# Two-layer conditioned sequence kernel: the second half of the next batch's query and key projection moved into a batch's last two half-steps

## The chip, the cores and the metric

The kernel runs on one core of a Trainium2 chip. The metric is the device time of one execution in microseconds (us); less is better. The engines are TensorE (PE, weight loads PEld), VectorE (DVE), ScalarE (ACT), GpSimd (POOL) and SyncE (SP, which here only issues DMAs). They run their own instruction streams and meet only at semaphores.

## The reference, cut to what matters

x is (8, 512, 256), the condition t is (8, 64). Two layers follow each other:

```python
# layer 0
scale = cond @ norm_w.T + 1.0
h = x * (scale * rsqrt(mean(x * x) + EPS))
val, gate = split(h @ up_w.T)
h = val * gelu(gate)
hq, wq = act_quant(h), weight_quant(down_w)
x = hq @ wq.T + x
# layer 1, attention: 16 heads of 16
n = gamma * rmsnorm(x) + beta
q, k, v = n @ W_q.T, n @ W_k.T, n @ W_v.T          # split into heads
x = x + a_alpha * (softmax(scale * q @ k.T) @ v) @ W_o.T
# layer 1, feed-forward
n = gamma * rmsnorm(x) + beta
x = x + f_alpha * (silu(n @ gate_w.T) * (n @ hidden_w.T) @ out_w.T + out_b)
```

## The kernel before

Every fp32 product outside layer 0's second one is made of three matmuls: each operand is split into a high part (rounded to fp32r) and a low part (the rest), and high x high, high x low and low x high are summed in PSUM (PARTS, L40). ScalarE writes the high parts, VectorE or GpSimd subtracts to get the low ones.

**Phase 1** (up to about 260 us) runs layer 0 over 32 tiles of 128 tokens, and leaves x and its normalised, transposed form (xa) in DRAM. It also makes the first half of batch 0's query and key stacks.

**Phase 2** is what the change touches. It goes over the 8 batches. The body of a batch is written once for each engine (`pe_batch`, `act_batch`, `dve_batch`, `pool_batch`, `sp_batch`); batch 0 is unrolled, batches 1 to 5 are a loop, 6 and 7 are unrolled. A batch has 32 half-steps (HALVES). In half-step h TensorE does (`excursion_pe`): two score matmuls of the batch (`score_pe`, L927) and, for maxima needed 11 half-steps later, one pair of raw score matmuls (`raw_pe`, L886), whose row maxima VectorE takes (`maximum_dve`, L894). The next raw pair waits until the last maximum is read. In even half-steps the four matmuls of values follow (`values_pe`, L946), which need ScalarE's exps (`exp_act`, L935) of the two half-steps before. A group of four heads takes 8 half-steps; its maxima go, negated, into rows of `q_stack` by 8 small DMAs (`shift_dve`, `shift_sp`).

Behind that a half-step does one or two entries of a table (`plan`, L1187): the attention of batch b is interleaved with the feed-forward of batch b - 1 and projections. Before the change the table of a looped batch is: half-step 0, query and key projection of the second half of this batch's heads (L812); 1 and 4, the two parts of v (L862); 2 and 3, the output product of batch b - 1's attention (`wo_pe`, L1007); 7, transposes of its normalised rows (`xf_pe`, L1075); 8 and 9, query and key projection of the first half for batch b + 1; 10 to 25, gate and hidden products alternating (L1113); 26 to 31, the output product (`out_pe`, L1157) in 8 half pieces of 12 matmuls. The last batch keeps the pieces of the last two of these half-steps for after its last values.

The table entries share two PSUM banks, `ab[0]` and `ab[1]`. Semaphores `pair_full` and `pair_free` count their uses; `uses` (L1207) works out which use each entry is, and every engine waits for that count.

A projection's result goes bank, ScalarE high part (`qk_act`, L819), VectorE low part (`qk_dve`, L826) into a staging buffer, and from there by 12 DMAs of 128 KB into `q_stack` and `k_stack`. The staging of the first half is in `split`, that of the second half in the last two slots of `hid`, which the feed-forward uses too (RESERVED, L794). SP issues 8 of the 12 DMAs, ScalarE's queue 4 (`stack_sp`, `stack_act`).

The chain between the output product and xf is: VectorE scales and adds the residual (L1017, L1027), ScalarE squares (L1034), VectorE the mean (L1041), GpSimd the power -1/2 (L1045), VectorE the four normalised rows (`normed_dve`, L1059), TensorE transposes, VectorE gamma and beta (L1085), ScalarE and GpSimd the parts (L1092, L1098). The next batch's input is split by ScalarE and GpSimd (L535, L549) at half-step 5. An engine does in half-step h the follow-up work of the table entries of h - 1. On VectorE the follow-ups that free a bank come ahead of the maximum, others behind it.

In batch 0 empty odd half-steps get three filler matmuls (`fill_pe`, L1227).

Of the kernel before, what the change touches and what calls it, by code (L numbers as in the profile page):

```python
# [5 lines left out]
def cond_seq_kernel(nc, x_tok, xT, condT, vec_wT, up_wT, down_wT, wqT, wkT, wvT, woT, gate_wT, hidden_wT,  # L6
# [40 lines left out]
    with ctx:  # L47
# [653 lines left out]
        def before_act(act, n):  # L701
# [9 lines left out]
            for w in range(2):  # L711
                if n == QK_AT[w] + 1:
                    act.wait_ge(alpha_stored, 16)
                    qk_act(act, 0, w, 0, psum[6 + w])
# [16 lines left out]
        def before_pe(pe, n):  # L731
# [4 lines left out]
            for w in range(2):  # L736
                if n == QK_AT[w]:
                    pe.wait_ge(par_ready, 2)
                    pe.wait_ge(alpha_done, 3)
                    qk_pe(pe, 0, 0, w, 0, psum[6 + w])  # L740
# [4 lines left out]
        def before_dve(dve, n):  # L745
# [8 lines left out]
            for w in range(2):  # L754
                if n == QK_AT[w] + 1:
                    qk_dve(dve, 0, w, 0, psum[6 + w])
# [37 lines left out]
        RESERVED = NH - 2  # L794
# [11 lines left out]
        def qk_pe(pe, c, m, w, use, bank=None):  # L806
            bank = ab[w] if bank is None else bank
            pe.wait_ge(q_in_low, credited(q_in_low, c + 1))
            pe.wait_ge(pair_free[w], credited(pair_free[w], use))
# [4 lines left out]
            last.then_inc(pair_full[w], 1)  # L814

        def qk_act(act, m, w, use, bank=None):
            bank = ab[w] if bank is None else bank
# [4 lines left out]
        def qk_dve(dve, m, w, n, bank=None):  # L822
            bank = ab[w] if bank is None else bank
            dve.wait_ge(qk_high, n + w + 1)
            high, low = staging(m, w)
            nc.vector.scalar_tensor_tensor(low, bank[:], SOFTMAX_SCALE if w == 0 else 1.0, high.bitcast(f32),  # L826
                                           ALU.mult, ALU.subtract).then_inc(pair_free[w], 1)


        def stack_dma(eng, m, w, half, r):  # L830
# [3 lines left out]
                          .bitcast(f32), staging(m, w)[part][64 * half:64 * half + 64, :].bitcast(f32)) \  # L834
                .then_inc(stacked[m], 16)

        def stack_sp(sp, m, uses, scores=None):

            for w, rows in ((0, range(ROWS // HD)), (1, range(ROWS // HD - 2))):
                sp.wait_ge(pair_free[w], credited(pair_free[w], uses[w] + 1))  # L840
                if scores is not None:
                    sp.wait_ge(score_full, scores)
                for r in rows:
# [3 lines left out]
        def stack_act(act, m, half, use, scores=None):  # L847

            act.wait_ge(pair_free[1], credited(pair_free[1], use + 1))
            if scores is not None:  # L850
                act.wait_ge(score_full, scores)
# [4 lines left out]
        def v_pe(pe, c, m, use):  # L856
            pe.wait_ge(q_in_low, credited(q_in_low, c + 1))
            pe.wait_ge(pair_free[m], credited(pair_free[m], use))
            for t in range(HALF):
                tok = (m * HALF + t) * P  # L860
                for i, (a, wp, k) in enumerate(PROJECTION):
                    last = nc.tensor.matmul(ab[m][:, t * D:(t + 1) * D], xa_part[a][:, k, tok:tok + P],  # L862
                                            wv[wp][:, k, :], start=(i == 0), stop=(i == 5))
            last.then_inc(pair_full[m], 1)
# [72 lines left out]
        def values_pe(pe, b, g, kt, v_use=None):  # L937

            if v_use is not None:
                m = kt // HALF  # L940
                pe.wait_ge(pair_free[m], credited(pair_free[m], v_use[m] + 1))
# [175 lines left out]
        def gate_act(act, c, f, use, spare=False):  # L1117
            act.wait_ge(pair_full[0], use + (f + 1))
            if f > 0:
                act.wait_ge(pair_free[1], credited(pair_free[1], use + f))  # L1120
# [7 lines left out]
        def product_dve(dve, c, f, use, spare=False):  # L1128
            dve.wait_ge(pair_free[0], credited(pair_free[0], use + (f + 1)))
            dve.wait_ge(prod_low, credited(prod_low, c * NH + f))  # L1130
            dve.wait_ge(pair_full[1], use + (f + 1))
# [3 lines left out]
        def product_act(act, c, f, use, staged):  # L1135
            if f == RESERVED:
                act.wait_ge(stacked[1], staged * STACK)
# [9 lines left out]
        def out_pe(pe, c, t, half, use):  # L1147
# [11 lines left out]
            if t % HALF == HALF - 1 and half == 1:  # L1159
                last.then_inc(pair_full[m], 1)  # L1160

        def out_dve(dve, c, m, use):
# [4 lines left out]
                                    fscale[:].unsqueeze(1).broadcast_to([P, HALF, D]), ALU.mult).then_inc(pair_free[m], 1)  # L1167
# [9 lines left out]
        V_AT, WO_AT, XF_AT, FFN_AT, OUT_AT = (1, 4), 2, 7, 10, 26  # L1177
        Q_AT, K_AT, TO_STACK = 8, 9, 16
# [438 lines left out]
```

## Time and profile before

| | |
|---|---|
| runs, median (lowest to highest) | 1056.83 us of 3 (1056.44 to 1062.42) |
| profiled execution, time | 1055.76 us |
| its span | 1054.0 us |
| TensorE busy | 996.8 us, 95% |
| VectorE busy | 761.7 us, 72% |
| ScalarE busy | 536.2 us, 51% |
| GpSimd busy | 269.4 us, 26% |
| share of TensorE's full clock granted, mean | 0.968 |

The busy times say how long an engine had an instruction in it; the matmuls are pipelined, so a busy TensorE may still be held up. The page's chain of waits, followed back from the end, lies on TensorE for 78% of the span and on VectorE for 12%. The median lies 1.07 us above the profiled execution's own time.

### The profile page before, as it was taken

Reading aid. Unit: us, or ns where it says so; the run is one execution under the profiler, and the core shown is the slowest. Engines: PE = TensorE matmul, PEld = TensorE weight load, DVE = VectorE, ACT = ScalarE, POOL = GpSimd, SP = SyncE. Lnnn points to the kernel's source line nnn. Section 1 sums busy time; section 2 is a strip of 40 time slices with the busy share of each in tenths; the row PEclk is TensorE's granted clock in tenths of the full one; section 3 lists DMA queues with packets and bytes.
Section 4 is the critical chain, followed back from the end, with each engine's and each line's share of the span. In section 5 each row is a group of like instructions: output and inputs, shape, how many; then the busy total and the mean of one; then the engine's idle time right before and its main releaser. Section 6 shows DMA issues by size and latency. Waiting matters only on the chain.

```text
span 1054.0 us, 17114 instructions
## 1 busy us (share of the span) xinstructions
PE 996.8 (95%) x5402; PEld 618.3 (59%) x5402; DVE 761.7 (72%) x1214; ACT 536.2 (51%) x1119; POOL 269.4 (26%) x258
## 2 busy tenths in 40 slices
PE   6999999996999899989989998999899899989988
PEld 4777777773534455645655564556456555645677
DVE  5888788996577777678677767776875877587233
ACT  5466455453555555456445545554564555356421
POOL 1365422221000312132122213221321232122142
PEclk9999999997999899989999998999899899999999
DMA  9544574432420240313022212403130222120000
GB/s 288 144 104 128 141 155 116 120 95 71 111 62 7 59 113 2 81 50 66 11 70 68 47 34 63 98 1 80 51 66 11 72 65 32 62 51 7 11 16 21
DMA packets 93718, 75.11 MB, mean 71 GB/s; under 512 B 44881, under 2 KB 79769, under 8 KB 93665
## 3 DMA queue, kind: packets, MB, share of 16 engines
q1 hardware_dynamic: 79072, 57.20, 20.9%
q10 hardware_dynamic: 14592, 17.25, 7.2%
q8 instruction: 27, 0.44, 0.2%
q14 instruction: 27, 0.21, 0.1%
HBM read 27.73 MB, written 12.61 MB: 38 GB/s over the span
## 4 chain that ended last, share of the span: by engine, by line
PE 78%; DVE 12%; issue 4%; DMA 2%; SPq 1%; ACT 1%; POOL 0%; DVEq 0%; ACTq 0%; POOLq 0%
PE bank L1113 19%; PE bank L362 12%; PE bank L927 10%; PE bank L946 10%; PE bank L1157 8%; PE raw_pair L886 6%; PE bank L812 4%; DVE rowmax L894 3%; PE bank L1007 2%; DVE amax L444 2%; PE bank L385 1%; PE bank L1075 1%; PE bank L862 1%; DVE h L414 1%; DVE x_in L1059 1%
## 5 line engine op out<-in xcount | busy, mean ns | idle before, releaser
L894 DVE TENSOR_REDUCE rowmax<-raw_pair 128x2 f32<-128x1024 f32 x256 | 312.9, 1222 | 127.7 <-PE raw_pair L886 127.7
L935 ACT ACTIVATE probs<-bank 128x512 f32<-128x512 f32 x512 | 281.8, 596 | 230.0 <-PE bank L927 227.7
L886 PE MATMUL raw_pair<-k_stack,q_stack 48*128 48x512 f32 x512 | 177.3, 472 | 24.5 <-DVE rowmax L894 23.7
L927 PE MATMUL bank<-q_stack,k_stack 50*128 50x512 f32 x512 | 197.3, 456 | 2.4 <-DMA q_stack<-shift_rows 1.3
L362 PE MATMUL bank<-up_w,xs_part 128*128 128x512 f32 x768 | 193.3, 405 | 5.7 <-issue 4.5
L362 PEld LDWEIGHTS bank<-up_w,xs_part 128*128 128x128 f32 x768 | 143.4, 192 | 40.5 <-issue 7.4
L946 PE MATMUL bank<-probs,v_ext 128*17 128x512 f32 x1024 | 139.5, 618 | 1.4 <-ACT probs L935 1.2
L1143 POOL TENSOR_TENSOR hid<-scratch,hid 128x512 fp32r<-128x512 f32 x64 | 82.4, 1287 | 217.2 <-ACT hid L1139 217.2
L927 PEld LDWEIGHTS bank<-q_stack,k_stack 50*128 50x128 f32 x512 | 81.7, 190 | 87.4 <-issue 50.3
L1113 PE MATMUL bank<-xf_part,gate_w 128*128 128x512 f32 x384 | 106.0, 411 | 0.8 <-POOL xf_part L1098 0.8
L1113 PE MATMUL bank<-xf_part,hidden_w 128*128 128x512 f32 x384 | 105.3, 409 | 0.0
L1113 PEld LDWEIGHTS bank<-xf_part,gate_w 128*128 128x128 f32 x384 | 68.2, 189 | 61.8 <-issue 48.5
L886 PEld LDWEIGHTS raw_pair<-k_stack,q_stack 48*128 48x128 f32 x512 | 71.3, 190 | 43.6 <-DVE rowmax L894 38.1
L1157 PEld LDWEIGHTS bank<-out_w,hid 128*128 128x128 f32 x672 | 80.5, 188 | 24.8 <-issue 24.8
L1157 PE MATMUL bank<-out_w,hid 128*128 128x256 f32 x672 | 88.7, 285 | 0.0
L1113 PEld LDWEIGHTS bank<-xf_part,hidden_w 128*128 128x128 f32 x384 | 67.7, 188 | 32.6 <-issue 20.3
L292 ACT ACTIVATE gelu<-bank,rstd 128x512 f32<-128x512 f32 x64 | 44.0, 688 | 58.0 <-PE bank L362 58.0
L1121 ACT ACTIVATE scratch<-bank 128x512 f32<-128x512 f32 x64 | 38.0, 594 | 65.1 <-PE bank L1113 65.1
L414 DVE SCALAR_TENSOR_TENSOR h<-bank,rstd,gelu 128x512 f32<-128x512 f32 x64 | 47.7, 746 | 23.1 <-PE bank L362 23.1
L340 POOL TENSOR_TENSOR xs_part<-xs,xs_part 128x256 fp32r<-128x256 f32 x32 | 23.6, 737 | 145.5 <-DVE ms L407 126.9
L1125 DVE SCALAR_TENSOR_TENSOR scratch<-scratch,bank 128x512 f32<-128x512 f32 x64 | 43.4, 679 | 17.6 <-ACT scratch L1121 17.6
L986 POOL TENSOR_TENSOR split<-o_sb,split 128x512 fp32r<-128x512 f32 x16 | 20.5, 1284 | 133.7 <-ACT split L982 133.7
(138 smaller groups left out, 1135.1 us busy)
## 6 DMA issues: line engine op xcount, KB each, us to landing
q_stack<-split SPq DMA_DIRECT2D x48, 128.0 KB, 3.0
q_stack<-hid SPq DMA_DIRECT2D x48, 128.0 KB, 2.9
xk<-xT SPq DMA_DIRECT2D x32, 128.0 KB, 3.0
xt<-x_tok SPq DMA_DIRECT2D x32, 128.0 KB, 2.7
x_spill<-x1t ACTq DMA_DIRECT2D x32, 128.0 KB, 2.5
xa_spill<-xa ACTq DMA_DIRECT2D x32, 128.0 KB, 2.3
x_in<-xa_spill SPq DMA_DIRECT2D x8, 512.0 KB, 4.8
k_stack<-split ACTq DMA_DIRECT2D x32, 128.0 KB, 4.8
```

What stands on the lines that cost most here:

```text
L292: nc.scalar.activation(gelu[:, j, :], gate_bank[j][:], ACT.Gelu, scale=rstd[:, m % 2:m % 2 + 1]) \
L362: last = nc.tensor.matmul(bank[j][:], xs_part[a][:, m % 2, k, :], up_w[w][:, k, col + j * W:col + (j + 1) * W], start=(i == 0), stop=(i == ...
L414: nc.vector.scalar_tensor_tensor(h[:, j * W:(j + 1) * W], val_bank[j][:], rstd[:, m % 2:m % 2 + 1], gelu[:, j, :], ALU.mult, ALU.mult) \
L886: mm = nc.tensor.matmul(raw_pair[:, half, :], q_stack[rows, slot, qt * P:(qt + 1) * P], k_stack[rows, slot, :], start=True, stop=True)
L894: nc.vector.reduce_max(rowmax[:, e:e + RAWS + 1:RAWS], raw_pair[:], AX.X).then_inc(raw_read, 1)
L927: nc.tensor.matmul(score_bank[c % 3][:], k_stack[rows, slot, kt * P:(kt + 1) * P], q_stack[rows, slot, :], start=True, stop=True).then_inc ...
L935: nc.scalar.activation(probs[:, (kt % 2) * J + j, :], score_bank[c % 3][:], ACT.Exp).then_inc(exp_done, 1)
L946: last = nc.tensor.matmul(o_bank[32 * j:32 * j + HD + 1, :], v_ext[:, kt, J * g + j, :], probs[:, (kt % 2) * J + j, :], start=(kt == 0), s ...
L1113: last = nc.tensor.matmul(work_bank(n, f, spare)[:], weight[wp][:, k, f * P:(f + 1) * P], xf_part[a][:, k, :], start=(i == 0), stop=(i == 5))
L1125: nc.vector.scalar_tensor_tensor(scratch[0][:], scratch[0][:], 1.0, work_bank(0, f, spare)[:], ALU.add, ALU.mult) \
L1143: nc.gpsimd.tensor_tensor(hid[1][:, f, :], scratch[1][:], hid[0][:, f, :].bitcast(f32), ALU.subtract) \
L1157: last = nc.tensor.matmul(ab[m][:, (t % HALF) * D:(t % HALF + 1) * D], hid[a][:, f, t * P:(t + 1) * P], out_w[wp][:, f, :], start=(i == 0) ...
```

## The change

- Query and key projection of the second half move from half-step 0 of a batch to half-steps 30 and 31 of the batch before, behind the output pieces, both in bank 0. Batch 0 has nothing before it and keeps its own two at half-step 0 ("own"). Both halves now use the same staging in `split`.
- The two parts of v move from half-steps 1 and 4 to 0 and 1, with swapped banks (V_BANK), and ScalarE copies them instead of VectorE (`v_act`).
- The first half's projections move from 8 and 9 to 4 and 8, xf from 7 to 6, the split of the next input from 5 to 2.
- The normalised rows are made by ScalarE with a scale per partition (`normed_act`), at half-step 5, and in the tail too.
- The output product's 8 half pieces are dealt differently over the same six half-steps. What the last batch keeps for after its last values is now 2 half pieces instead of 3.
- SP issues all 12 stack DMAs in phase 2, those of the second half at the end of its program for the batch, between the stores of the two output halves. ScalarE issues none there.
- The fillers of batch 0 stand where the new table leaves odd half-steps empty, except half-step 5.
- The counting of the banks' uses becomes a pair, one number for each bank.

```diff
-        def split_xa_act(act, c, v_use=None):
+        def split_xa_act(act, c):
             act.wait_ge(xa_loaded, (c + 1) * 16)
-            if v_use is not None:
-                for m in range(2):
-                    act.wait_ge(pair_free[m], credited(pair_free[m], v_use[m] + 1))
...
-        def staging(m, w):
-            if m == 0:
-                return split[:, 2 + w, :], split[:, 6 + w, :]
-            return hid[0][:, RESERVED + w, :], hid[1][:, RESERVED + w, :]
+        def staging(w):
+            return split[:, 2 + w, :], split[:, 6 + w, :]
...
-        def qk_act(act, m, w, use, bank=None):
-            bank = ab[w] if bank is None else bank
-            act.wait_ge(pair_full[w], use + 1)
-            nc.scalar.activation(staging(m, w)[0], bank[:], ACT.Copy, scale=SOFTMAX_SCALE if w == 0 else 1.0) \
+        def qk_act(act, w, n, use, bank=None, other=None):
+            bank = ab[n] if bank is None else bank
+            act.wait_ge(pair_full[n], use + 1)
+            if other is not None:
+                act.wait_ge(stacked[other[0]], other[1] * STACK)
+            nc.scalar.activation(staging(w)[0], bank[:], ACT.Copy, scale=SOFTMAX_SCALE if w == 0 else 1.0) \
                 .then_inc(qk_high, 1)
...
-        def v_dve(dve, c, m, use):
-            dve.wait_ge(pv_done, credited(pv_done, c * 16))
-            dve.wait_ge(pair_full[m], use + 1)
-            nc.vector.tensor_scalar(v_ext[:, m * HALF:(m + 1) * HALF, :, 0:HD],
-                                    ab[m][:].rearrange("p (t h d) -> p t h d", t=HALF, d=HD), 1.0, None, ALU.mult) \
-                .then_inc(pair_free[m], 1)
+        def v_act(act, c, m, use):
+            n = V_BANK[m]
+            act.wait_ge(pv_done, credited(pv_done, c * 16))
+            act.wait_ge(pair_full[n], use + 1)
+            nc.scalar.activation(v_ext[:, m * HALF:(m + 1) * HALF, :, 0:HD],
+                                 ab[n][:].rearrange("p (t h d) -> p t h d", t=HALF, d=HD), ACT.Copy) \
+                .then_inc(pair_free[n], 1)
...
-        def normed_dve(dve, c, rows=None, normed=None):
-            dve.wait_ge(rstd3_done, c + 1)
+        def normed_act(act, c, rows=None, normed=None):
+            act.wait_ge(rstd3_done, c + 1)
             for t in range(T):
-                last = nc.vector.tensor_scalar((normed or normed_rows)(t), (rows or x2)[:, t, :], rstd3[:, t:t + 1], None, ALU.mult)
+                last = nc.scalar.activation((normed or normed_rows)(t), (rows or x2)[:, t, :], ACT.Copy,
+                                            scale=rstd3[:, t:t + 1])
             last.then_inc(xn3_done, 1)
...
-        V_AT, WO_AT, XF_AT, FFN_AT, OUT_AT = (1, 4), 2, 7, 10, 26
-        Q_AT, K_AT, TO_STACK = 8, 9, 16
-        SPLIT_XA_AT = V_AT[1] + 1
-        OUT_PIECES = ([(0, 0)], [(2, 0)], [(0, 1)], [(1, 0), (1, 1)], [(2, 1)], [(3, 0), (3, 1)])
+        V_AT, WO_AT, XF_AT, FFN_AT, OUT_AT = (0, 1), 2, 6, 10, 26
+        QK0_AT, QK1_AT, TO_STACK = (4, 8), (30, 31), 16
+        SPLIT_XA_AT, NORMED_AT = V_AT[1] + 1, WO_AT + 3
+        V_BANK = (1, 0)
+        OUT_PIECES = ([(0, 0)], [(2, 0)], [(0, 1), (1, 0)], [(1, 1), (2, 1)], [(3, 0)], [(3, 1)])
...
-            table[0] = [("qk", 1, 0), ("qk", 1, 1)]
+            if not ffn:
+                table[0] = [("own", 0), ("own", 1)]
             for m in range(2):
-                table[V_AT[m]] = [("v", m)]
-            if following:
-                table[Q_AT] = [("qk", 0, 0)]
-                table[K_AT] = [("qk", 0, 1)]
+                table[V_AT[m]] += [("v", m)]
...
+            if following:
+                for w in range(2):
+                    table[QK0_AT[w]] += [("qk0", w)]
+                    table[QK1_AT[w]] += [("qk1", w)]
...
-                if not ffn and not table[h] and h % 2 == 1:
+                if not ffn and not table[h] and h % 2 == 1 and h != QK0_AT[0] + 1:
                     fill_pe(pe, h, u, at)
...
+                    elif p[0] == "own":
+                        qk_act(act, p[1], p[1], both(u, at["own"])[p[1]], None, (0, 1))
+                    elif p[0] == "qk0":
+                        qk_act(act, p[1], p[1], both(u, at["qk0"])[p[1]], None, (1, b + 1))
+                    elif p[0] == "qk1":
+                        qk_act(act, p[1], 0, u[0] + at["qk1"] + p[1], None, (0, b + 2))
+                    elif p[0] == "v":
+                        v_act(act, b, p[1], both(u, at["v"])[V_BANK[p[1]]])
...
-                if h in (2, 3):
-                    stack_act(act, 1, h - 2, u + at["qk1"][1])
...
+                if ffn and h == NORMED_AT:
+                    normed_act(act, b - 1)
...
-                if following and h in (TO_STACK, TO_STACK + 1):
-                    stack_act(act, 0, h - TO_STACK, u + at["qk0"][1], b * 64 + 32)
...
-                if ffn and h == WO_AT + 3:
-                    normed_dve(dve, b - 1)
                 for p in done:
                     if p[0] == "gate":
                         gate_dve(dve, b - 1, p[1])
-                    elif p[0] == "qk" and p[1] == 0:
-                        qk_dve(dve, 0, p[2], 4 * b + 4)
+                    elif p[0] == "qk0":
+                        qk_dve(dve, p[1], p[1], 4 * b + 4)
+                    elif p[0] == "qk1":
+                        qk_dve(dve, p[1], 0, 4 * b + 6)
...
-                if h == 0:
-                    qk_dve(dve, 1, 0, 4 * b + 2)
...
         def sp_batch(sp, b, u, ffn, following):
-            stack_sp(sp, 1, both(u, at["qk1"]))
+            if not ffn:
+                stack_sp(sp, 1, enumerate(both(u, at["own"])))
...
             if ffn:
-                sp_store(sp, b - 1)
+                sp_store(sp, b - 1, 0)
+            if following:
+                stack_sp(sp, 1, [(0, u[0] + at["qk1"] + w) for w in range(2)])
+            if ffn:
+                sp_store(sp, b - 1, 1)
```

## Rows read from the trace of the kernel before

**Rows 1.** The windows: length, then busy of PE, PEld, DVE, ACT, POOL; PEclk, DMA share, GB/s.

```profile
260.80:335.74 74.94, 72.98 (x339) 32.27 (x339) 49.20 (x60) 41.86 (x71) 3.64 (x2) 0.96 0.26 63
335.74:432.70 96.96, 94.29 (x528) 53.61 (x528) 70.07 (x93) 50.01 (x97) 22.36 (x16) 0.95 0.20 52
432.70:911.33 478.63, 460.31 (x2642) 264.43 (x2642) 353.38 (x465) 249.73 (x485) 118.82 (x85) 0.96 0.22 53
...
939.20:942.50 3.30, 3.30 (x13) 1.32 (x13) 2.87 (x2) 0.60 (x1) 1.46 (x1) 0.50 0.70 220
```

**Rows 2.** The waits of PE in batch 3: total, times, longest.

```profile
PE raw_pair L886 <- DVE rowmax L894: 3.6, 2, 2.2
```

**Rows 3.** The timeline of PE, batch 3 to its first gate product.

```profile
528.76 0.49 PE L927 MATMUL bank<-q_stack,k_stack 50*128 50x512 f32 x1
...
551.65 0.88 PE L886 MATMUL raw_pair<-k_stack,q_stack 48*128 48x512 f32 x2 [2.23 <-DVE rowmax L894]
...
562.81 1.66 PE L1113 MATMUL bank<-xf_part,gate_w 128*128 128x512 f32 x6
```

**Rows 4.** The timeline of DVE, the same batch, half-steps 6 to 8.

```profile
547.20 3.26 DVE L1059 TENSOR_SCALAR x_in<-x,rstd 128x256 f32<-128x256 f32 x4
...
555.11 1.53 DVE L1085 TENSOR_SCALAR x_in<-bank,par 128x512 f32<-128x512 f32 x2 [0.95 <-PE bank L1075]
```

**Rows 5.** The timeline of DVE, batch 7.

```profile
929.44 1.14 DVE L1059 TENSOR_SCALAR x_in<-x,rstd 128x256 f32<-128x256 f32 x4
...
937.22 1.23 DVE L894 TENSOR_REDUCE rowmax<-raw_pair 128x2 f32<-128x1024 f32 x1 [0.23 <-PE raw_pair L886]
```

**Rows 6.** The timeline of POOL, batch 3.

```profile
546.16 1.01 POOL L1045 TENSOR_TENSOR rstd<-ms,minus_half 128x4 f32<-128x4 f32 x1 [9.24 <-DVE ms L1041]
...
547.51 2.53 POOL L549 TENSOR_TENSOR xa_part<-x_in,xa_part 128x1024 fp32r<-128x1024 f32 x1 [0.35 <-ACT xa_part L535]
```

**Rows 7.** The timeline of PE, the end of batch 3.

```profile
610.89 0.50 PE L927 MATMUL bank<-q_stack,k_stack 50*128 50x512 f32 x1
...
611.55 1.05 PE L946 MATMUL bank<-probs,v_ext 128*17 128x512 f32 x8
...
612.53 1.63 PE L1157 MATMUL bank<-out_w,hid 128*128 128x256 f32 x12
...
614.09 0.49 PE L927 MATMUL bank<-q_stack,k_stack 50*128 50x512 f32 x1
...
621.63 3.09 PE L1157 MATMUL bank<-out_w,hid 128*128 128x256 f32 x24
...
624.65 0.50 PE L927 MATMUL bank<-q_stack,k_stack 50*128 50x512 f32 x1
```

**Rows 8.** The timeline of PE, batch 7, half-steps 7 to 10.

```profile
932.43 1.09 PE L1075 MATMUL bank<-ident,x_in 128*128 128x128 f32 x8
...
936.42 0.50 PE L886 MATMUL raw_pair<-k_stack,q_stack 48*128 48x512 f32 x2 [0.41 <-DVE rowmax L894]
...
938.50 0.50 PE L886 MATMUL raw_pair<-k_stack,q_stack 48*128 48x512 f32 x2 [1.34 <-DVE rowmax L894]
...
939.17 1.91 PE L946 MATMUL bank<-probs,v_ext 128*17 128x512 f32 x8
...
941.01 2.37 PE L1113 MATMUL bank<-xf_part,gate_w 128*128 128x512 f32 x6
```

**Rows 9.** One line's instructions: the low part of a projection, ns min/median/max.

```profile
L826 DVE SCALAR_TENSOR_TENSOR hid<-bank,hid x16: 691/692/692, 265.5 to 916.7; 128x512 fp32r<-128x512 f32 x16
```

**Rows 10.** One line's instructions, ns min/median/max: scaled copy; square.

```profile
L309 ACT ACTIVATE xs<-xk,par x64: 385/391/405, 5.5 to 233.1; 128x128 f32<-128x128 f32 x64
...
L1034 ACT ACTIVATE scratch<-x x28: 398/409/418, 349.6 to 926.6; 128x256 f32<-128x256 f32 x28
```

**Rows 11.** The timeline of SP's queue, batch 3.

```profile
533.45 3.84 SPq L833 DMA_DIRECT2D q_stack<-hid  x6
```

**Rows 12.** One line's instructions: the divide's multiplication, ns min/median/max.

```profile
L968 DVE TENSOR_TENSOR o_pair<-o_tok,inv_sum x32: 424/425/2299, 290.2 to 999.5; 128x256 f32<-128x256 f32 x32
```

More of the change, by code:

```diff
@@ L833, in stack_dma, with stack_sp, stack_act @@
             eng.dma_start((q_stack, k_stack)[w][64 * half + r:64 * half + ROWS:ROWS // HD, G * m:G * m + G, :]
-                          .bitcast(f32), staging(m, w)[part][64 * half:64 * half + 64, :].bitcast(f32)) \
+                          .bitcast(f32), staging(w)[part][64 * half:64 * half + 64, :].bitcast(f32)) \
                 .then_inc(stacked[m], 16)
-        def stack_sp(sp, m, uses, scores=None):
-            for w, rows in ((0, range(ROWS // HD)), (1, range(ROWS // HD - 2))):
-                sp.wait_ge(pair_free[w], credited(pair_free[w], uses[w] + 1))
+        def stack_sp(sp, m, ready, scores=None):
+            for w, (n, use) in enumerate(ready):
+                sp.wait_ge(pair_free[n], credited(pair_free[n], use + 1))
                 if scores is not None:
                     sp.wait_ge(score_full, scores)
-                for r in rows:
+                for r in range(ROWS // HD):
                     for half in range(2):
                         stack_dma(sp, m, w, half, r)
-        def stack_act(act, m, half, use, scores=None):
+        def stack_act(act, m, half, use):
             act.wait_ge(pair_free[1], credited(pair_free[1], use + 1))
-            if scores is not None:
-                act.wait_ge(score_full, scores)
             for r in range(ROWS // HD - 2, ROWS // HD):
@@ L1144, in product_pool, with out_pe @@
                 .then_inc(prod_low, 1)
-        def out_pe(pe, c, t, half, use):
+        def out_pe(pe, c, t, half, use, count=1):
             m = t // HALF
@@ L1237, in cond_seq_kernel, with uses_before @@
         USES_FIRST, USES_LOOP = uses(False, 2)[1], uses(True, 2)[1]
+        def uses_before(b):
+            return tuple((b - 1) * USES_LOOP[n] + (BEFORE + USES_FIRST[n]) for n in range(2))
         def last_of(b, g):
@@ L1272, in pe_batch @@
                     elif p[0] == "out":
-                        out_pe(pe, b - 1, p[1], p[2], u + at["out"])
-                    else:
-                        hidden_pe(pe, b - 1, 0 if p[0] == "gate" else 1, p[1], u + at["hidden"])
+                        m = p[1] // HALF
+                        out_pe(pe, b - 1, p[1], p[2], both(u, at["out"])[m], out_count(m, following))
+                    else:
+                        n = 0 if p[0] == "gate" else 1
+                        hidden_pe(pe, b - 1, n, p[1], both(u, at["hidden"])[n])
         def act_batch(act, b, u, ffn, following):
             table, at = plan(ffn, following), uses(ffn, following)[0]
-            for h in range(HALVES):
+            for h in range(HALVES + 1):
                 g, kt = h // 2 // T, h // 2 % T
@@ L1326, in dve_batch @@
                     elif p[0] == "hidden":
-                        product_dve(dve, b - 1, p[1], u + at["hidden"])
+                        product_dve(dve, b - 1, p[1], both(u, at["hidden"]))
                     elif p[0] == "out" and p[1] % HALF == HALF - 1 and p[2] == 1:
-                        out_dve(dve, b - 1, p[1] // HALF, u + at["out"])
+                        m = p[1] // HALF
+                        out_dve(dve, b - 1, m, both(u, at["out"])[m], out_count(m, following))
                 if ffn and h == WO_AT + 3:
@@ L1378, in pool_batch @@
                     elif p[0] == "out" and p[1] % HALF == HALF - 1 and p[2] == 1:
-                        out_pool(pool, b - 1, p[1] // HALF, u + at["out"])
+                        out_pool(pool, b - 1, p[1] // HALF, both(u, at["out"])[p[1] // HALF])
         def sp_x1(sp, c):
@@ L1416, in sp_batch @@
             if following:
-                stack_sp(sp, 0, both(u, at["qk0"]), b * 64 + 32)
+                stack_sp(sp, 0, enumerate(both(u, at["qk0"])), b * 64 + 32)
             if ffn:
@@ L1547, in phase2_program @@
             before(eng)
-            batch(eng, 0, BEFORE, False, 2)
+            batch(eng, 0, (BEFORE, BEFORE), False, 2)
             with eng.Fori(0, B - 3) as i:
-                batch(eng, i + 1, i * USES_LOOP + (BEFORE + USES_FIRST), True, 2)
+                batch(eng, i + 1, tuple(i * USES_LOOP[n] + (BEFORE + USES_FIRST[n]) for n in range(2)), True, 2)
             for n in range(2):
-                batch(eng, B - 2 + n, BEFORE + USES_FIRST + (B - 3 + n) * USES_LOOP, True, 1 - n)
+                batch(eng, B - 2 + n, uses_before(B - 2 + n), True, 1 - n)
             after(eng)
```

163 lines of the change are left out of this document (83 added, 80 removed).

## The prediction

> **What bounds the kernel now.** I read the windows first, cut at the first score of each batch [rows 1]. In the five looped batches TensorE is busy 460.31 of 478.63 us, so matmul work sets the pace and an edit pays only where it takes out idle or half-clock time. A looped batch lasts 478.63 / 5 = 95.7 us, batch 1 96.96, batch 0, which has no feed-forward work, 74.94. The waits of TensorE [rows 2] say where the idle is: 3.6 us in batch 3, two stalls, the longer 2.2, both for VectorE's row maximum. The timeline [rows 3] puts the long one at half-step 7, before the raw pair; the other, 1.4, is at 6. VectorE's own rows name the cause [rows 4]: the four normalised rows take 3.26 us, and the next maximum queues behind them. They took 1.14 in batch 7 [rows 5]. What differs is GpSimd, which from 547.51 runs a 2.53 us subtraction [rows 6]. In batch 3 it takes 562.81 - 528.76 = 34.05 us from the first score to the first gate matmul [rows 3].
>
> **Prices at full clock.** From the end of batch 3 [rows 7]: a half-step's scores and raw pair 0.66 (610.89 to 611.55), values 0.98, one projection or half output piece before a score 1.56 to 1.6, two together 3.02. The transposes of xf take about 1.03 (a row of 1.09) [rows 8]. So an even half-step with one block is 3.24, an odd one 2.26. A half-step without a block is not 0.66: a raw pair needs the last maximum read. With no more than a transpose beside it on VectorE two raw pairs stand 938.50 - 936.42 = 2.08 apart [rows 8]; the maximum starts 0.80 after its raw pair and frees the next 1.28 after its own start (936.42, 937.22, 938.50) [rows 5, 8]. Other VectorE work between them adds to it.
>
> **The change, part by part,** in a looped batch, with 0 at its first score.
> Half-step 0 loses two projections; the values projection v of half-step 1 comes in their place, and that of 4 comes to 1. Half-steps 0 to 4 are then 3.26, 2.28, 3.6, 2.26 and 3.24. The 3.6 holds a wait of 0.4: the second key projection's low part (0.69) [rows 9] is now ahead of the maximum of 0, the maximum of 1 starts behind sums, divide and turn at about 4.65, and the raw pair of 2 waits until 5.93. The half-steps start at 0, 3.3, 5.5, 9.2, 11.4, 14.7. The output product of 2 wants to start at 7.6; its input comes through ScalarE and GpSimd at 6.9, a cover of 0.6.
> The v copies leave VectorE (two of some 0.7, as rows 9) for ScalarE, which is busy 249.73 of 478.63 [rows 1]. I cost them there at nothing: what hides them is that an exp is needed only two scores later.
> The normalised rows on ScalarE: each has a scale per partition. A 128x128 copy with one takes 391 ns, a 128x256 square without one 409 [rows 10]. Bounds for four: 4 x 0.41 less overlaps, 1.35, and 2.0. I take 1.74, the 128x128 row and 0.12 for the further columns, less overlap, as that is the row nearest in kind. VectorE gets the first product at 9.4, then the maximum of 3, sum, product and sum at 0.6 to 0.7 each: the second sum ends at 13.3. Two squares end at 14.7, the mean and GpSimd's power (1.01) [rows 6] at 16.4, the rows run from 16.45 to 18.2. The transposes can start at 18.4, behind half-step 6's values: a cover of 0.2, so this chain is nearly critical.
> Half-steps 5, 7 and 9 have no block now. The maximum of 4 starts at 13.2, behind that second sum, and has shift and mean after it, so the maximum of 5 starts at 15.5 and raw pair 6 at 16.8: a stall of 1.3 where 1.4 stood. Half-step 7 starts at 19.4. Its maximum queues behind the 1.53 us of gamma and beta [rows 4], starts at 21.1 and lets raw pair 8 go at 22.4, where half-step 8 could start at 20.1. That is a new stall of 2.1. The key projection of the first half then fills 8, and raw pair 10 waits 1.3 again. The first gate comes at 29.4 against 34.05: 4.65 gained, if the clock holds.
> Given back at the end: half-step 28 takes two pieces, 0.66 + 0.98 + 3.02 = 4.66, 29 takes 3.6, 30 a piece and the query projection 4.65. At 31 the key projection has the same bank: it waits until VectorE has read the query, 0.8 + 1.14 (maximum) + 0.69 after the half-step's start, 0.5 late, and ends at 4.3. Together 17.2 against 624.65 - 610.89 = 13.8 [rows 7]: 3.4 lost.
> Net 1.2 gained, a length of 94.5. Batches 1 to 6 took 96.96 + 478.63 = 575.6 and would take 567.2: -8.4.
> Queues. SP issues 12 stack DMAs a half instead of 8 and ScalarE's queue none. Six took 3.84 us [rows 11], so those of the second half are out at some 6 us, and their reader is half-step 5 at 14.7: 8.7 us for the last to land. The output store behind them has until 12.6, when the residual is rewritten. The eight shift DMAs of group 1 go out after 15.2; no row here gives their landing, but up to 7.2 us the stall at 8 covers it. All three cost nothing; without cover the late one moves half-step 8.
> Batch 0 pays: in half-step 0 v waits for the bank of the key projection just before it (1.5 for its block, 1.5 for the high and low part that free the bank: +3.0), 4 and 8 are shorter (-1.3), 30 and 31 carry the new projections (+1.1, +2.0): +4.8.
> Batch 7 has no following one. Its gate comes 2.4 earlier, less 1.6 as one more output piece stands before the last values [rows 7]: -0.8. The tail's rows cost 1.74 for 1.14 [rows 5]: +0.6.
> Sum at full clock: -8.4 + 4.8 - 0.8 + 0.6 = -3.8.
>
> **The clock.** Batch 7 before has stalls like these: after gaps of 0.41 and 1.34 us, 1.7 apart, the granted clock was 0.50 [rows 1, 8], the lower of its levels, 1.2 GHz. Values then took 1.91 for 1.05 and a gate block 2.37 for 1.66 [rows 3, 7, 8]: 1.6 lost. The changed batch has stalls of 1.3, 2.1 and 1.3. Bounds: no fall, 0; one in each of batches 1 to 7, 7 x 1.6 = 11. I take five, nearer the upper end since the 2.1 is longer than either gap of batch 7: +8. That makes +4.2 on the profiled run's 1055.76 (span 1054.0), which stands 1.1 below the median: 1060.
> The Trainium skill (TensorE: Matmul & The Clock Gate, section Why this matters for your kernels) lets the clock fall after one long idle gap between bursts; by it the short gaps here would cost nothing and the time would be 1052. The two short gaps of batch 7 speak against it.
>
> **The rivals.**
> 1. The forecast: the gain of half-steps 0 to 9 is eaten by 28 to 31, batch 0 and the clock. 1056 to 1066. Chance 0.42.
> 2. The clock holds in nearly every batch: 1060 - 8 = 1052, 1050 to 1055. For it, the work between the stalls is denser than in batch 7; against it, the 2.1 at half-step 8. Chance 0.20.
> 3. Faster: VectorE's residual work and the maxima interleave better than I queued them, the stalls are half as long, and the clock holds. Half of 1.3 + 2.1 + 1.3 is 2.3, times 6 is 14, so 1038 from 1052, up to 1045. Against it: the spacing of 2.08 is measured. Chance 0.18.
> 4. Slower, one mechanism: the chain from half-step 2's products through squares, mean, power and ScalarE's rows reaches the transposes late. ScalarE's line now holds a v copy, the turned outputs, the next input's split, the squares and a projection's high part. It decides from 0.2 us of lateness; at 0.8 the stall at 6 grows by 0.6 and the clock falls twice a batch, 1.6 more: 6 x 2.2 = 13, 1073. The split stands at half-step 2 now, so its 2.53 us on GpSimd [rows 6] end at 11.0, 0.2 before a residual sum wants to start on VectorE. Of the divide's multiplications, which also read two SBUF tensors, the longest took 2.30 us against 0.43 [rows 12]. Chance 0.17.
> The Trainium skill (SBUF — State Buffer, section SBUF: two separate sides) says that such an instruction is blocked for the whole of GpSimd's; no run here shows it for this sum.
> 5. It relieves nothing, since maxima wait for raw pairs anyway: 1056. Chance 0.03.
>
> **How the numbers follow.** About 1% (1046.3 to 1067.4) is what a measurement of this kernel can tell from no change. Faster is rival 3 and a little of 2, 0.20. Slower is rival 4 and the edge of the forecast, 0.19. Within is the rest, 0.61. The range 1044 to 1070 leaves out the far parts of 3 and 4, 0.2.
>
> **What would show it.** Right: a looped batch of 94 to 97 us; stalls before raw pairs 6, 8 and 10 of 1.3, 2.1 and 1.3; a wait of 0.5 in half-step 31; the first gate 29 to 31 us after the first score; half-steps 28 to 31 at 17.2; batch 0 near 80. Wrong: no window at 0.50 in batches 2 to 6 (rival 2), transposes that wait for ScalarE (rival 4), a wait for stack DMAs at half-step 5, or a store that delays the residual.

## The result, and the profile after

The changed kernel takes 1076.88 us (median of 4 runs, 1070.85 to 1081.84) against 1056.63 before: a ratio of 1.0183, 95% interval 1.0127 to 1.024. It is slower by 1.8%, where 1060 in a range of 1044 to 1070 was forecast. The profiled execution took 1076.17, its span is 1074.4 against 1054.0.

The windows of the changed kernel, cut at the first score of each batch as in [rows 1], two short ones in batch 3, one in batch 2 and three in batch 4 (length, busy of PE, PEld, DVE, ACT, POOL, then PEclk). The third is five batches long, as in [rows 1]; they are batches 2 to 6, of which the last is unrolled with the same table, and "looped" here means these five:

```profile
262.62:343.30 80.68, 74.30 (x348) 33.50 (x349) 48.79 (x59) 43.26 (x74) 3.65 (x2) 0.96 0.19 60
343.30:441.10 97.80, 93.06 (x530) 52.80 (x530) 66.22 (x87) 52.23 (x103) 23.33 (x17) 0.97 0.16 51
441.10:930.80 489.70, 467.19 (x2643) 265.86 (x2642) 331.08 (x435) 261.32 (x515) 118.03 (x86) 0.96 0.16 52
562.20:565.40 3.20, 3.20 (x13) 1.69 (x6) 1.65 (x2) 0.27 (x1) 2.87 (x2) 0.50 0.30 67
569.00:572.20 3.20, 3.20 (x13) 1.53 (x6) 1.28 (x2) 0.35 (x1) 0.00 (x0) 0.50 0.02 7
463.10:469.90 6.80, 6.27 (x19) 2.90 (x21) 2.41 (x3) 1.51 (x4) 4.48 (x3) 0.50 0.42 128
654.30:657.60 3.30, 3.30 (x18) 1.93 (x12) 0.91 (x1) 1.11 (x3) 0.00 (x0) 0.50 0.02 3
661.10:664.40 3.30, 3.30 (x12) 1.33 (x7) 1.94 (x2) 0.58 (x1) 3.30 (x2) 0.50 0.18 52
667.90:671.30 3.40, 3.40 (x13) 1.43 (x13) 1.58 (x3) 0.60 (x1) 0.00 (x0) 0.50 0.04 15
```

Against [rows 1], batch 0 is 80.68 - 74.94 = 5.7 longer, batch 1 0.8, the five looped ones 489.70 - 478.63 = 11.1 together, 2.2 each: 17.6 of the 20.4 us. Phase 2 also starts 1.8 later, in code that the change leaves alone (the changed kernel with fillers, below, starts it at 260.20, as early as before), and batch 7 with the tail makes up the rest of the 20.4. VectorE did 22 us less in the five batches and ScalarE 11.6 more, as meant; TensorE's busy time rose by 6.9 with the same matmuls. More busy time for the same work is a sign of a slower clock, or of longer gaps inside groups.

Where a looped batch loses, the timeline of TensorE in batch 3 shows (start and length in us, idle before and its releaser in brackets). The counterparts of before are in [rows 3, 8]:

```profile
555.36 0.59 PE L886 MATMUL raw_pair<-k_stack,q_stack 48*128 48x512 f32 x2 [1.12 <-DVE rowmax L894]
...
557.02 1.09 PE L1076 MATMUL bank<-ident,x_in 128*128 128x128 f32 x8
...
559.18 0.49 PE L927 MATMUL bank<-q_stack,k_stack 50*128 50x512 f32 x1 [0.41 <-DMA q_stack<-shift_rows]
561.11 0.59 PE L886 MATMUL raw_pair<-k_stack,q_stack 48*128 48x512 f32 x2 [1.44 <-DVE rowmax L894]
...
561.76 1.65 PE L946 MATMUL bank<-probs,v_ext 128*17 128x512 f32 x8
563.35 2.62 PE L809 MATMUL bank<-xa_part,wk 128*128 128x512 f32 x6
...
567.98 0.58 PE L886 MATMUL raw_pair<-k_stack,q_stack 48*128 48x512 f32 x2 [1.12 <-DVE rowmax L894]
...
568.65 1.70 PE L946 MATMUL bank<-probs,v_ext 128*17 128x512 f32 x8
570.28 2.58 PE L1114 MATMUL bank<-xf_part,gate_w 128*128 128x512 f32 x6
```

The stalls stand before raw pairs 6, 8 and 10, of 1.1, 0.4 + 1.4 and 1.1. Each of the five batches has three; the waits of TensorE over 441 to 931 us say so (total, times, longest):

```profile
PE raw_pair L886 <- DVE rowmax L894: 19.3, 15, 2.1
```

In batch 3, behind the second and the third, values and the block after them run at 0.50 of the clock: 1.65 and 2.62 where a full clock gives 1.05 and 1.66, and again 1.70 and 2.58. The first gate comes at 570.28, 31.7 us after the batch's first score at 538.57, against 34.05. Worked out were 29.4. A stretch at half clock is called a fall below. Falls do not stand in the same place in every batch: batches 1 and 5 have one behind the stall before raw pair 6 (17.4 to 17.6 us from the first score) and one at 24.3, batch 4 has three, and batches 2 and 6 have a single one twice as long. Each batch of 1 to 6 so spends 6.8 us at half clock, batch 4 10.2. The next rows are VectorE's in the same stretch, and one of ScalarE's:

```profile
554.08 1.23 DVE L894 TENSOR_REDUCE rowmax<-raw_pair 128x2 f32<-128x1024 f32 x1 [0.37 <-PE raw_pair L886]
555.23 0.68 DVE L825 SCALAR_TENSOR_TENSOR split<-bank,split 128x512 fp32r<-128x512 f32 x1
556.18 1.23 DVE L894 TENSOR_REDUCE rowmax<-raw_pair 128x2 f32<-128x1024 f32 x1 [0.27 <-PE raw_pair L886]
558.40 1.53 DVE L1086 TENSOR_SCALAR x_in<-bank,par 128x512 f32<-128x512 f32 x2 [0.99 <-PE bank L1076]
559.85 1.21 DVE L894 TENSOR_REDUCE rowmax<-raw_pair 128x2 f32<-128x1024 f32 x1
```

```profile
554.90 1.71 ACT L1059 ACTIVATE x_in<-x,rstd 128x256 f32<-128x256 f32 x4
```

The 3.26 us of [rows 4] are gone. The maximum at 559.85 queues behind gamma and beta: the new stall. The four rows on ScalarE end at 556.61, 0.4 before the transposes start. At the batch's end and in batch 0, two waits for a bank:

```profile
634.79 1.67 PE L809 MATMUL bank<-xa_part,wk 128*128 128x512 f32 x6 [0.36 <-DVE split L825]
```

```profile
270.50 1.67 PE L861 MATMUL bank<-wv,xa_part 128*128 128x256 f32 x12 [1.50 <-DVE split L825]
```

### The profile page after: what moved, and what is told of

Read it like the earlier page. It is cut to its first block, busy times and chain, and to the rows that moved or that the text cites. A ratio compares the mean times of both kernels' runs of the same rounds, so it can differ in the third digit from the quotient of the medians.

```text
span 1074.4 us, 17150 instructions
## 1 busy us (share of the span) xinstructions
PE 1002.0 (93%) x5399; PEld 617.7 (57%) x5399; DVE 728.8 (68%) x1166; ACT 554.4 (52%) x1167; POOL 268.6 (25%) x258
## 4 chain that ended last, share of the span: by engine, by line
PE 82%; DVE 10%; issue 3%; DMA 2%; SPq 1%; ACT 1%; POOL 0%; DVEq 0%; ACTq 0%; POOLq 0%
PE bank L1114 19%; PE bank L946 12%; PE bank L362 12%; PE bank L927 11%; PE bank L1156 7%; PE raw_pair L886 6%; PE bank L809 5%; DVE rowmax L894 3%; PE bank L861 2%; PE bank L1007 2%; DVE amax L444 2%; PE bank L385 1%; DVE h L414 1%; PE bank L1076 1%; PE bank L393 1%
## 5 line engine op out<-in xcount | busy, mean ns | idle before, releaser
L886 PE MATMUL raw_pair<-k_stack,q_stack 48*128 48x512 f32 x512 | 175.1, 466 | 30.7 <-DVE rowmax L894 30.3
L927 PE MATMUL bank<-q_stack,k_stack 50*128 50x512 f32 x512 | 192.4, 449 | 3.5 <-DMA q_stack<-shift_rows 1.9
L946 PE MATMUL bank<-probs,v_ext 128*17 128x512 f32 x1024 | 144.9, 640 | 1.2 <-ACT probs L935 1.2
L1126 DVE SCALAR_TENSOR_TENSOR scratch<-scratch,bank 128x512 f32<-128x512 f32 x64 | 43.4, 678 | 17.6 <-ACT scratch L1122 17.6
```

The costliest lines, as they stand in the source:

```text
L886: mm = nc.tensor.matmul(raw_pair[:, half, :], q_stack[rows, slot, qt * P:(qt + 1) * P], k_stack[rows, slot, :], start=True, stop=True)
L927: nc.tensor.matmul(score_bank[c % 3][:], k_stack[rows, slot, kt * P:(kt + 1) * P], q_stack[rows, slot, :], start=True, stop=True).then_inc ...
L946: last = nc.tensor.matmul(o_bank[32 * j:32 * j + HD + 1, :], v_ext[:, kt, J * g + j, :], probs[:, (kt % 2) * J + j, :], start=(kt == 0), s ...
```

## The experiments

The runs ask where the 2.2 us a batch went, and what each part of the change does by itself. Theory A: the gain at full clock is nil or a small loss, and the clock, which falls twice a batch behind the new stalls, makes the rest. Fillers are matmuls whose result nobody reads, into the score bank that the next score overwrites. Ratios are to the kernel before, run beside each of them.

**The changed kernel with fillers at its stalls.**

```diff
+        STALL_FILLS = {5: 4, 7: 7, 9: 4}
+        def fill_stall_pe(pe, b, h, count):
+            c = 2 * (h + 1)
+            pe.wait_ge(exp_done, credited(exp_done, b * 64 + (c - 2)))
+            for i in range(count):
+                nc.tensor.matmul(score_bank[c % 3][:], wo[0][:, i % GP, 0:P],
+                                 wo[1][:, 0:2, :].rearrange("p g n -> p (g n)"), start=(i == 0), stop=(i == count - 1))
...
                     ... # last in a half-step of pe_batch
+                if ffn and h in STALL_FILLS:
+                    fill_stall_pe(pe, b, h, STALL_FILLS[h])
```

> The changed kernel with filler matmuls on TensorE at the end of half-steps 5, 7 and 9 of batches 1 to 7 (4, 7 and 4 of 512 columns, into the bank that the next score overwrites), where its stalls are 1.1, 1.9 and 1.1 us. They add no useful work. Theory A (the clock falls twice a batch behind these stalls, and that is the 3.3 us by which a batch is longer than the 94.5 I worked out): no stretch at 0.50 between batch 1 and 6, batches of 94.5 to 95, 1077 - 7 x 3.3 = 1054 to 1057 us. Theory B (the low clock costs little and the time is in the order of the work itself): 1074 to 1078 us, with the fillers only taking the place of idle time.

1055.26 us, ratio 1.0001 [0.998, 1.0023]. Adding 15 useless matmuls a batch takes 2% off the changed kernel. The window over its five looped batches, and the first gate product of batch 3, whose first score is at 530.16:

```profile
435.53:908.36 472.83, 470.55 (x2717) 271.56 (x2717) 330.51 (x435) 261.77 (x515) 118.27 (x86) 1.00 0.17 54
```

```profile
559.62 1.65 PE L1114 MATMUL bank<-xf_part,gate_w 128*128 128x512 f32 x6
```

A batch takes 472.83 / 5 = 94.6 us at a granted clock of 1.00; without fillers 97.9. So the clock costs 3.4 us a batch, and the rest of the working, which gave 94.5, stands: the first gate product comes 29.5 us after the first score, where 29.4 were worked out. Theory B falls.

**The kernel before with fillers** (the same edit, with {5: 5, 6: 7}).

> The kernel before with fillers at its own stalls, 5 at the end of half-step 5 and 7 at the end of 6. Theory A: its clock fall of 6.8 us a batch, worth 2.3, goes too: batches of 93.3, 1056 - 16 = 1038 to 1043 us; so the changed kernel's base of 94.5 is worse than this one's, and the change has no gain in it once the clock is taken out. Theory B: 1054 to 1058 us.

1043.58 us, 0.9888 [0.9869, 0.9907], 0.6 above the top of theory A's range. Its window, and the first gate product of batch 3 (first score at 523.26):

```profile
429.36:898.51 469.15, 466.69 (x2701) 270.00 (x2700) 355.04 (x465) 250.69 (x485) 118.95 (x85) 1.00 0.22 54
```

```profile
555.37 1.65 PE L1113 MATMUL bank<-xf_part,gate_w 128*128 128x512 f32 x6
```

93.8 us a batch for 95.7: a lower price, 1.9, than the changed kernel's 3.4 (theory A had 2.3). With the clock out of both, the change loses (472.83 - 469.15) / 5 = 0.7 us a batch and the rest in batch 0. It has no gain hidden under the clock. At full clock the first gate product of before comes at 32.1 and not at 34.05, so half-steps 0 to 9 gain 2.6, and 28 to 31 lose 3.3.

**The changed kernel with the fillers of half-step 7 alone** ({7: 7}).

> The changed kernel with the 7 fillers at half-step 7 alone, where the new stall of 1.9 us stands; the stalls of 1.1 before raw pairs 6 and 10 stay idle. Theory A1 (that one stall starts both falls of the clock, the second because the first drags the idle of half-steps 8 to 10 along): few falls or none, 1054 to 1060 us. Theory A2 (each stall brings its own fall): about one fall a batch left, 1063 to 1069 us.

1060.79 us, 1.0055 [1.0036, 1.0075]. Its looped batches and one short window in batch 3:

```profile
440.58:918.26 477.68, 464.11 (x2676) 266.92 (x2676) 330.69 (x435) 261.65 (x515) 118.23 (x86) 0.99 0.17 53
554.50:557.70 3.20, 3.20 (x16) 1.57 (x8) 1.11 (x1) 1.32 (x3) 0.00 (x0) 0.50 0.02 3
```

The time lies between the two theories' ranges, 0.8 above the first. Some 4 us of it stand in batch 0, which the edit leaves alone: in the profiled execution it had two falls and took 84.50 us, where the changed kernel took 80.68. By their first scores batches 1 and 4 took 94.7, and 2, 3 and 5 96.2 to 96.3; each of those three holds one stretch at half clock, the two short ones none. So one fall costs 1.5 to 1.6 us here, as I had read from batch 7. Batches 2 to 6 spend 10.2 us at half clock, where the changed kernel spends 37.6: with the stall at half-step 8 filled most of the falls are gone, but not all. Stalls of 1.1 us bring one in one batch and none in the next.

**The order alone**: the changed kernel with both copies back on VectorE (`v_dve`, `normed_dve` as before, and the split waits for v's banks again).

```diff
-                    elif p[0] == "v":
-                        v_act(act, b, p[1], both(u, at["v"])[V_BANK[p[1]]])
...
-                if ffn and h == NORMED_AT:
-                    normed_act(act, b - 1)
...
+                    elif p[0] == "v":
+                        v_dve(dve, b, p[1], both(u, at["v"])[V_BANK[p[1]]])
...
+                if ffn and h == NORMED_AT:
+                    normed_dve(dve, b - 1)
```

> The changed order alone: v copies and normalised rows back on VectorE, everything else as changed (the split of the next input waits for the v copies again). Theory A (the order makes three half-steps without a block and three stalls, whoever copies): 1074 to 1082 us, with two falls of the clock a batch. Rival (ScalarE's longer line is what makes the changed kernel slow): 1050 to 1065 us.

1077.34 us, 1.0198 [1.0166, 1.023], the changed kernel's time. ScalarE's longer line is not what makes it slow. The four rows on VectorE:

```profile
555.96 1.13 DVE L1062 TENSOR_SCALAR x_in<-x,rstd 128x256 f32<-128x256 f32 x4
```

They take 1.13 us here, not 3.26: with the split at half-step 2, GpSimd's subtraction is over before. In the new order the move to ScalarE had little left to save: the whole of the change's loss is in its order.

**The assignment**: the kernel before with the normalised rows on ScalarE, then with the v copies as well, order and split kept.

```diff
+                if ffn and h == WO_AT + 3:
+                    normed_act(act, b - 1)
                 if ffn and h == XF_AT + 1:
...
-                if ffn and h == WO_AT + 3:
-                    normed_dve(dve, b - 1)
```

> The kernel before with one part of the change: the four normalised rows on ScalarE (in the tail too), at half-step 5 behind the split; v and the order stay. Theory A: the 2.2 us stall at half-step 7 goes, since the maximum of 6 no longer queues behind 3.26 us; transposes 2.8 us earlier, the stall at 6 stays at 1.4 and one fall of the clock may stay with it: batches of 91 to 93, 1027 to 1040 us. Rival (ScalarE's line is full at half-step 5, so that rows and transposes come late): within 5 us of 1056.

1037.73 us, 0.9835 [0.9815, 0.9856]: 1.6% faster than before by this one part. In its batch 3 one stall is left:

```profile
PE raw_pair L886 <- DVE rowmax L894: 1.4, 1, 1.4
```

It stands before raw pair 6; the one at 7, 2.2 in [rows 2, 3], is gone.

> The kernel before with both copies of the change on ScalarE, the v copies and the normalised rows, and its order kept: the assignment alone, the counterpart of the order alone. Theory A: as with the rows alone (1038), less the 0.6 us by which a v copy on VectorE delays the maximum of half-step 5, so stalls of 0.9 instead of 1.5 before raw pair 6: 1030 to 1036 us. Rival (a v copy in ScalarE's line delays exps, squares and rows by as much): 1037 to 1042 us.

1034.38 us, 0.9816 [0.9798, 0.9833]. The v copies add at most a little: the intervals of the two ratios overlap, and the stall before raw pair 6 is 1.1 for 1.4, where 0.9 was expected. Batch 3 has no fall and takes 91.6; batches 2, 4 and 5 have one each and take 92.3. So a fall costs only 0.7 here: what one costs depends on what runs in it.

**The same two with fillers** ({5: 4, 6: 3} and {5: 3, 6: 3}).

> The kernel before with the normalised rows on ScalarE and fillers at its stalls (4 at the end of half-step 5, 3 at 6). Theory A: the gains of the two edits add up but for the clock time that both remove: batches of 91.7 without a fall (as batches 2 and 4 of the run without fillers), 1038 - 7 x 1.4 = 1026 to 1031 us. Rival (the fillers delay the chain as much as they save): 1035 to 1040 us.

1032.73 us, 0.9791 [0.9772, 0.9811]: 2 us above what theory A gave, and better than the rival. Filled, a batch is 92.1, not the 91.7 of an unfilled one without a fall.

> The same with fillers at its stalls, 3 at the end of half-step 5 and 3 at 6. Theory A: no fall of the clock in batches 1 to 6 and batches of 91 to 91.7, against 92.1 with the rows alone and fillers: 1024 to 1031 us, the fastest so far. Rival: 1032 to 1036 us, no better than the rows alone with fillers.

1030.35 us, 0.978 [0.9759, 0.98]. This is the fastest kernel here, 2.2% below the one before and some 4% below the changed one. Its looped batches:

```profile
427.46:885.82 458.36, 458.14 (x2671) 263.63 (x2671) 333.65 (x435) 261.80 (x515) 118.33 (x85) 1.00 0.22 56
```

91.7 us each, with TensorE busy in all of it.

**The move of the second half alone**: both copies on ScalarE and the previous places for all else. With it come the dealing of the output pieces, the shared staging and SP's issuing of all stack DMAs, as in the change; the order of the banks' uses follows, not shown.

```diff
-        V_AT, WO_AT, XF_AT, FFN_AT, OUT_AT = (0, 1), 2, 6, 10, 26
-        QK0_AT, QK1_AT, TO_STACK = (4, 8), (30, 31), 16
+        V_AT, WO_AT, XF_AT, FFN_AT, OUT_AT = (1, 4), 2, 7, 10, 26
+        QK0_AT, QK1_AT, TO_STACK = (8, 9), (30, 31), 16
-        V_BANK = (1, 0)
+        V_BANK = (0, 1)
```

> The previous order (v at 1 and 4, transposes at 7, first-half projections at 8 and 9, split at 5) and both copies on ScalarE, but with the second half's projections in half-steps 30 and 31 of the batch before and the output pieces dealt as changed: against the kernel with both on ScalarE it differs by the move alone, without fillers. Theory A (the move takes 2.5 off half-step 0, whose length becomes that of the maxima's turn of 2.1, and puts 3.4 on 28 to 31, and batch 0 pays some 3): 6 to 12 us slower than that kernel, 1038 to 1046 us. Rival (the move is worth its 2.5 and costs nothing at the end): 5 to 15 us faster, 1018 to 1028 us.

1049.62 us, 0.9966 [0.9952, 0.998], against 1034.38 without the move: 15 us slower, 3 more than the range I gave theory A. The rival falls. By first scores, half-steps 0 to 3 of batch 3 take 1.65, 3.26, 4.27 and 2.26, together 11.4 where they took 12.8; so half-step 0 gives back 1.3 and not 2.5, since 1 and 2 now wait for the maxima. 28 to 31 cost 3.3 more, and batch 0 is 78.8 for 74.5. From here to the changed kernel, 1076.88, it is another 27 us: these lie in the new places of v, the transposes, the first half's projections and the split.

**The blocks in odd half-steps**: the changed kernel with first-half projections at 5 and 9 and the transposes at 7. The fillers of batch 0 follow.

```diff
-        V_AT, WO_AT, XF_AT, FFN_AT, OUT_AT = (0, 1), 2, 6, 10, 26
-        QK0_AT, QK1_AT, TO_STACK = (4, 8), (30, 31), 16
+        V_AT, WO_AT, XF_AT, FFN_AT, OUT_AT = (0, 1), 2, 7, 10, 26
+        QK0_AT, QK1_AT, TO_STACK = (5, 9), (30, 31), 16
```

> The changed kernel with its three blocks in the odd half-steps: first-half projections at 5 and 9 instead of 4 and 8, transposes at 7 instead of 6. Same work, same engines, no fillers. Theory A (the loss is three half-steps without a block and the falls behind their stalls): half-steps 4 to 9 take about 13 instead of 16.4, batches of 91 to 92.5, no falls, 1028 to 1038 us, 4% below the changed kernel. Rival (the loss is in the four blocks put into half-steps 30 and 31 and in batch 0): 1070 to 1077 us.

1041.19 us, 0.9866 [0.9848, 0.9885]: some 3% below the changed kernel, 3 us above the range. The same work without a filler:

```profile
433.58:896.99 463.41, 454.53 (x2641) 260.71 (x2640) 339.70 (x435) 261.13 (x515) 118.23 (x86) 1.00 0.17 55
```

92.7 us a batch, and the clock holds in these five. Half-steps 4 to 9 take 14.3 in batch 3, for 16.4 in the changed kernel, not 13. Of the 5.2 us a batch that three entries moved by one slot bring, 3.4 are the clock's and 1.9 are there at full clock too (94.6 against 92.7).

**The same idea in the kernel before**: rows on ScalarE, and the second part of v at 5 instead of 4.

```diff
-        V_AT, WO_AT, XF_AT, FFN_AT, OUT_AT = (1, 4), 2, 7, 10, 26
+        V_AT, WO_AT, XF_AT, FFN_AT, OUT_AT = (1, 5), 2, 7, 10, 26
```

> The kernel before with the normalised rows on ScalarE and the second part of v moved from half-step 4 to 5 (and the next split from 5 to 6). A half-step with values and no block takes 1.64 of TensorE, one with a block and no values 2.26, and both are near the 2.08 between two raw pairs; a block beside the values makes 3.24 and leaves the next at 0.66, which then stalls. Theory A: half-steps 4 to 7 take 2.1, 2.26, 2.1, 2.1 to 2.5 instead of 10.5 together, batches of 89 to 90, no falls, 1012 to 1022 us. Rival (the maxima or the chain to the transposes set the pace of half-steps 4 to 7 whatever the order): 1028 to 1038 us.

1042.35 us, 0.9875 [0.9855, 0.9895], a miss: 4.6 us slower than with v at 4, outside both ranges. VectorE's and TensorE's rows in batch 3 say why:

```profile
549.39 1.53 DVE L1086 TENSOR_SCALAR x_in<-bank,par 128x512 f32<-128x512 f32 x2 [1.83 <-POOL xa_part L549]
```

```profile
550.98 2.93 PE L812 MATMUL bank<-xa_part,wq 128*128 128x512 f32 x6 [1.63 <-DVE x_in L1086]
```

The split of the next input follows v, so it went from 5 to 6 and GpSimd's part of it is late. Gamma and beta overwrite the buffer that it reads and wait 1.83, and the next projection waits 1.63 for their bank. I had not looked for what reads `x_in`. In the run above v, and with it the split, is early, and gamma and beta do not wait there.

## Why the prediction was wrong

The step that failed is the clock, "Bounds: no fall, 0; one in each of batches 1 to 7, 7 x 1.6 = 11. I take five falls". The size of a fall was about right: 1.5 to 1.6 us by batches with and without one in the kernel with fillers at 7. Their number was not. The changed kernel has two falls in each of batches 1, 3 and 5, three in batch 4, and one of double length in 2 and 6. By the first scores batches 1 to 6 take 587.5 us, and 567.5 with fillers: the clock cost 20 us, where I had 8 for all. The upper bound was no bound: it took one fall a batch as given, though three stalls were worked out, and the rival that had two falls a batch tied them to a late chain that did not come.

The whole difference of the profiled times, 20.4 us, is then this: batches 1 to 6 at full clock -8.1 (-8.4 forecast), the clock in them +20 (+8), batch 0 +5.7 (+4.8), batch 7 and the tail +1.0 (-0.2), and +1.8 of start.

A second error did not move the sum, but it hid the reason. The "4.65 gained, if the clock holds" and the "Sum at full clock: -3.8" compare the changed batch at full clock with a batch of before that had 6.8 us at half clock itself; [rows 1] give 0.96 for its window. In batch 3 it was here:

```profile
550.10:556.80 6.70, 5.15 (x23) 2.72 (x23) 4.41 (x7) 1.87 (x4) 0.00 (x0) 0.50 0.00 0
```

```profile
552.80 1.97 PE L1075 MATMUL bank<-ident,x_in 128*128 128x128 f32 x8
```

With the clock out of both, half-steps 0 to 9 gain 2.6 and not 4.65, less than the 3.3 that 28 to 31 lose. The edit had no gain a batch to begin with: the 1.2 of the working is the 1.9 that before's own fall costs, less 0.7.

The other steps, each against its rows:

- **The order at full clock.** 94.5 worked out, 94.6 measured with fillers. The starts of half-steps 0 to 5, the stalls before raw pairs 6, 8 and 10 (1.3, 2.1, 1.3 forecast; 1.1, 1.9, 1.1 shown) and half-steps 28 to 31 (17.2; 636.40 - 619.3 = 17.1) all came as said.
- **The tail of a batch.** The wait for bank 0 in half-step 31 was there, 0.36 of idle where 0.5 was forecast; the half-step took 4.28, as said. It is a true cost of putting both projections in one bank.
- **Batch 0.** 4.8 forecast, 5.7 measured; v's wait for the key projection's bank is 1.50.
- **ScalarE's rows.** 1.74 forecast, 1.71 measured. The cover of 0.2 was 0.4, and rival 4, the late chain, did not occur: no transpose waited. The order alone on VectorE takes the same time.
- **The collision of sum and subtraction**, part of rival 4: the split's 2.39 us on GpSimd end before the residual's sum starts, and each of the latter's instructions took 0.68 to 0.69. So it did not show, and what it would cost these two stays untried. The split's move did end the old collision, 1.13 for 3.26 with the rows on VectorE.
- **Queues.** No wait for stack DMAs or stores. The shift rows kept a score 0.41 us, inside the stall, as said.
- **The long gap.** That only a long gap lets the clock fall would have given 1052. Stalls of 1.1 to 1.9 us, with work between them, were enough, and none in the five batches was longer than 2.1. The Trainium skill (TensorE: Matmul & The Clock Gate, section Why this matters for your kernels) warns of long idle gaps between bursts; read as the prediction reads it, that shorter ones cost nothing, it does not hold in this kernel.
- **Rival 3** (stalls half as long) and **rival 2** (the clock holds) fall with the trace. Rival 2's 1052 was nearly the time of the kernel with fillers, 1055.

What the 2.2 us a looped batch are made of: +0.7 at full clock, and 3.4 for the clock instead of 1.9. That before's price is lower although its time at half clock was as long I read from what ran in it: there TensorE was busy 5.15 of 6.70 us, with a stall and transposes among it, in batch 3 of the changed kernel all of it, with values, projection and gate products. No run separates that further. The fillers may themselves cost a little, so the prices are lower bounds: with the rows on ScalarE a filled batch took 0.4 more than an unfilled one without a fall. In the changed kernel they seem to cost nothing, 94.6 with 15 of them and 94.7 with 7.

One part of the change is good and was drowned: the rows on ScalarE, -17.7 us in the old order. The moved second half costs 15 us in that order.

## What to carry to other kernels

Where two instructions on TensorE take turns with one on another engine, a slot without other work is not free time saved: it takes the period of that turn, 2.1 us here, and the idle in it can lower the clock for the dense work behind. Spread blocks so that each slot is near that period (92.7 against 97.9 us a batch by moving three entries by one slot), or fill the idle, and when bounding a clock loss count every stall as a candidate. Before a forecast at full clock, take the half-clock stretches out of the kernel before as well. Before moving an entry, list what its follow-ups overwrite: with v at 5 it was a buffer, not an engine, that the loss came from.

## What the runs showed of the hardware

- Useless matmuls made a kernel faster: 15 a batch took some 21 us off. Without fillers the granted clock was 0.50 in batch 3 behind the stalls of 0.4 + 1.4 us before raw pair 8 and 1.1 before raw pair 10; with them it was 1.00 over all five looped batches.
- Whether stalls of 1.1 us bring a fall varies from batch to batch in the same run (94.7 or 96.2 us for the same program), and one fall cost 1.5 to 1.6 us in one kernel and 0.7 in another. The changed kernel's runs lie 11 us apart (1070.85 to 1081.84). Fillers do not end that by themselves: the filled one ranges from 1051.48 to 1060.51, its slowest run at a mean granted clock of 0.981 and its fastest at 0.990.
- Four scaled copies of 128x256 took 1.14 us on VectorE alone, 3.26 beside a GpSimd subtraction, and 1.71 on ScalarE; 1.70 there beside a GpSimd subtraction of 2.36 (the kernel before with the rows on ScalarE).
